# Attention of sixteen sequences: the slots of all engines in a new order

## What is computed

```python
cq = rms_norm(hidden_states @ w_qa.T, q_a_ln_w)                    # 192 columns
q = (cq @ w_qb.T).reshape(b, s, H, DQ).transpose(0, 2, 1, 3)       # 16 heads of 128 + 64
q_pe = q_pe * cos + rotate_half(q_pe) * sin
...
scores = jnp.einsum('bhqd,bhkd->bhqk', q_full, k_full) * scale
attn = jax.nn.softmax(jnp.where(causal, -jnp.inf, scores), axis=-1)
out = jnp.einsum('bhqk,bhkd->bhqd', attn, v)
return out @ w_o.T
...
x = _layernorm(x + rwkv_attention(x)); x = _layernorm(x + quantized_ffn(x))
x = _layernorm(x + latent_attention(x)); x = _layernorm(x + mixture_of_experts(x))
```

## Time and profile before

| | |
|---|---|
| median of 3 runs | 2410.62 us (2408.71 to 2412.27) |
| the profiled execution | 2416.53 us, span 2414.8 us |
| mean granted TensorE clock | 0.904 |
| TensorE, VectorE, ScalarE, GpSimd busy | 84%, 68%, 43%, 32% of the span |
| the attention phase, from its first scores to the next phase's first load | 1094.31 to 2054.26 us |

### The profile page before, as it was taken

The page is one execution under the profiler, slowest core; times in us unless marked ns, Lnnn a source line. Parts: engine busy times, 40 slices in busy tenths (PEclk is TensorE's granted clock), DMA queues, the critical chain, the costliest instruction groups (busy, mean ns, idle before and its releaser), DMA issues. The chain is left out here.

```text
span 2414.8 us, 36391 instructions
## 1 busy us (share of the span) xinstructions
PE 2026.7 (84%) x12368; PEld 1797.3 (74%) x12368; DVE 1650.5 (68%) x4500; ACT 1029.0 (43%) x2673; POOL 780.7 (32%) x701
## 2 busy tenths in 40 slices
PE   7999999999999699879998888888888884677850
PEld 5788878778787588748888888887888874567740
DVE  7876776677775465527788888888888885235428
ACT  5433433333332233226655555555555552225530
POOL 1222223222232000013344444444444445003552
PEclk9999999999999799969999999999998997788655
DMA  3100000000000344340000000000000000414656
GB/s 122 44 27 27 1 27 1 27 27 1 27 18 1 118 140 140 99 147 6 14 26 29 18 17 17 16 15 15 16 15 15 11 12 14 126 35 93 145 86 204
DMA packets 105975, 117.24 MB, mean 49 GB/s; under 512 B 17879, under 2 KB 97819, under 8 KB 105152
## 3 DMA queue, kind: packets, MB, share of 16 engines
q1 hardware_dynamic: 93504, 106.80, 14.3%
q0 software_dynamic: 12288, 8.11, 2.3%
HBM read 75.44 MB, written 55.53 MB: 54 GB/s over the span
## 5 line engine op out<-in xcount | busy, mean ns | idle before, releaser
L209 POOL TENSOR_TENSOR rwkv_gate<-rwkv_key,rwkv_gate 128x512 f32<-128x512 f32 x128 | 205.8, 1608 | 566.3 <-DVE rwkv_key L391 566.3
L1162 POOL TENSOR_TENSOR mla_w_raw<-mla_w_raw,mla_row_inv 128x512 f32<-128x512 f32 x192 | 199.1, 1037 | 351.4 <-DVE mla_row_inv L1478 350.6
L1293 ACT ACTIVATE mla_w_raw<-mla_w_raw,mla_least 128x256 f32<-128x256 f32 (+1 forms) x512 | 227.4, 446 | 85.6 <-DVE mla_least L1462 62.2
L276 ACT ACTIVATE rwkv_gate<-rwkv_r 128x512 f32<-128x512 f32 x128 | 76.4, 597 | 416.6 <-DVE rwkv_o_low L328 416.6
L377 DVE TENSOR_TENSOR rwkv_kv<-rwkv_v,rwkv_key 128x512 f32<-128x512 f32 x128 | 88.0, 688 | 176.5 <-PE rwkv_v L426 117.3
L1462 DVE CUSTOM_DVE_ANT_0 mla_w_raw<-mla_score,mla_mask 128x256 f32<-128x256 f32 (+1 forms) x512 | 156.5, 351 | 47.3 <-PE mla_score L1845 47.2
L443 PE MATMUL rwkv_out<-rwkv_w_high,rwkv_o_high 128*128 128x256 f32 x512 | 144.9, 283 | 35.6 <-DVE rwkv_o_low L328 35.6
L383 DVE TENSOR_TENSOR_SCAN rwkv_state<-rwkv_decay_w,rwkv_kv 128x256 f32<-128x256 f32 x256 | 163.4, 681 | 4.1
L1845 PE MATMUL mla_score<-mla_k_high,mla_q_high 128*128 128x256 f32 (+1 forms) x512 | 158.1, 309 | 0.0
L2200 POOL DMA_INDIRECT sums<-moe_y_rows,moe_e_rows x64 | 92.2, 1440 | 203.7 <-ACT moe_y_rows L2277 142.7
L1309 ACT ACTIVATE mla_p_high<-mla_turn 128x512 fp32r<-128x512 f32 x192 | 112.9, 588 | 84.5 <-PE mla_turn L1854 83.0
(11 more groups left out here) (371 smaller groups left out, 6647.1 us busy)
## 6 DMA issues: line engine op xcount, KB each, us to landing
moe_w_raw<-in_experts SPq DMA_DIRECT2D x32, 384.0 KB, 3.8
rwkv_w_raw<-in_rkvo SPq DMA_DIRECT2D x16, 512.0 KB, 3.3
moe_y_in<-sums SPq DMA_DIRECT2D x32, 256.0 KB, 3.0
sums<-ffn_empty SPq DMA_DIRECT2D x14, 512.0 KB, 7.8
slots<-ffn_empty SPq DMA_DIRECT2D x8, 722.5 KB, 6.4
moe_e_rows<-slots SPq DMA_DIRECT2D x32, 180.6 KB
mla_w_raw<-in_mla_heads SPq DMA_DIRECT2D x4, 1280.0 KB, 7.3
rwkv_x_in<-in_x_t SPq DMA_DIRECT2D x16, 256.0 KB, 4.3
```

The lines of the kernel that those rows point to most:

```text
L209: nc.gpsimd.tensor_tensor(gate[:, c % 2, :], key[:, c % 2, :], gate[:, c % 2, :], ALU.mult).then_inc(gated_done, 1)
L1162: nc.gpsimd.tensor_tensor(unit, unit, row_inv[:, v % PR, 0:len(heads)].rearrange("p (h a) -> p h a", a=1) .to_broadcast([P, len(heads), ke ...
L1293: last = nc.scalar.activation(probs[:, v % PR, i * keys:(i + 1) * keys], masked[:, v % 2, i * keys:(i + 1) * keys], ACT.Exp, bias=least[:, ...
```

## The change

The same instructions run per sequence, in another order. Each turn in `TURNS` may now carry the mark `late`. TensorE does in a slot: the probability turn, the scores, the early turns, the weighted sums, the late turns, and last the projection. What ScalarE, VectorE and GpSimd do with a late turn or a projection, they do at the start of the next slot (`late_turns`, `projected`). The latents move from slots 8 and 9 to 8 and 10, read in slots 9 and 11. The router's transposes and logits come one sequence later (`routed` and `logits`: -2), its 26 steps stand in slots 3 to 11, and the scatters in slots 0 to 7 of the sequence after. y1 moves to slot 8, y0 to slot 10, layer norm to slots 9 to 11. The residual rows and the rows of the sum (`x_res`, `y_rows`) have two buffers each. The loop runs over one sequence more.

```diff
-TURNS = (("q1", 0, 0), ("q1", 1, 1), ("q1", 2, 2), ("q1", 3, 3), ("k", 0, 3), ("q0", 0, 4), ("q0", 1, 5),
-         ("y1", 0, 5), ("q0", 2, 6), ("places", 0, 6), ("x", 0, 7), ("q0", 3, 9), ("routed", 0, 9), ("cq", 0, 10),
-         ("logits", 0, 11), ("y0", 0, 11))
-AHEAD = {"q1": 0, "k": 1, "q0": 1, "x": 2, "cq": 2, "y0": 0, "y1": -1, "routed": -1, "logits": -1, "places": -2}
+TURNS = (("q1", 0, 0), ("routed", 0, 0, "late"), ("q1", 1, 1), ("q1", 2, 2), ("logits", 0, 2, "late"), ("q1", 3, 3),
+         ("k", 0, 4), ("q0", 0, 5), ("q0", 1, 6), ("q0", 2, 7), ("x", 0, 7, "late"), ("q0", 3, 8),
+         ("y1", 0, 8, "late"), ("places", 0, 9, "late"), ("y0", 0, 10, "late"), ("cq", 0, 11, "late"))
+AHEAD = {"q1": 0, "k": 1, "q0": 1, "x": 2, "cq": 2, "y0": 0, "y1": -1, "routed": -2, "logits": -2, "places": -2}
 UNSPLIT = ("y0", "y1", "places")
 FIRST_TURNS = (("x", 0, 0), ("cq", 0, 0), ("k", 0, 0), ("x", 0, 1), ("q0", 0, 0), ("q0", 1, 0), ("q0", 2, 0),
                ("q0", 3, 0), ("cq", 0, 1))
-def slot_turns(seq, v):
-
-    return [(kind, index, seq + AHEAD[kind]) for kind, index, at in TURNS
-            if at == v and 0 <= seq + AHEAD[kind] < NSEQ and (seq < NSEQ or AHEAD[kind] < 0)]
+def slot_turns(seq, v, late):
+
+    return [(kind, index, seq + AHEAD[kind]) for kind, index, at, *when in TURNS
+            if at == v and (when == ["late"]) == late and 0 <= seq + AHEAD[kind] < NSEQ
+            and (seq < NSEQ or AHEAD[kind] < 0)]
 def turned_in(m):
@@ -883,8 +884,10 @@
 ALL_TURNS = list(FIRST_TURNS)
-for of_slot in range(SLOTS * (NSEQ + 2)):
-    ALL_TURNS += turned_in(of_slot) + slot_turns(*divmod(of_slot, SLOTS))
+for of_slot in range(SLOTS * (NSEQ + 3)):
+    ALL_TURNS += turned_in(of_slot)
+    for is_late in (False, True):
+        ALL_TURNS += slot_turns(*divmod(of_slot, SLOTS), is_late)
 TURN_AT = {t: n for n, t in enumerate(ALL_TURNS)}
 SPLITS = [sum(t[0] not in UNSPLIT for t in ALL_TURNS[:n + 1]) for n in range(len(ALL_TURNS))]
...
@@ -1041,6 +1044,19 @@
             return not isinstance(seq, int) or seq > 0
+        def late_turns(seq, v):
+
+            return slot_turns(*divmod(SLOTS * seq + v - 1, SLOTS), True) if seq + v > 0 else []
+
+        def projected(seq, v):
+
+            of, at = divmod(SLOTS * seq + v - 1, SLOTS)
+            if of < 0 or not exists(of + (1 if at < 8 else 2)) or at in (9, 11):
+                return None, None
+            if at < 8:
+                return ("abs" if at % 4 < 2 else "pe"), 8 * (of + 1) + at
+            return "latent", 2 * (of + 2) + (at - 8) // 2
+
         def slot_before(seq, v, back):
...
@@ -1116,12 +1132,12 @@
                     sp.wait_ge(turn_filled, TURN_AT["x", 0, seq + 1] + 1)
                     sp.dma_start(x_rows[:, :, :], seq_rows(x2, seq + 2)).then_inc(rows_in, 16)
-                if v == 9 and exists(seq):
-                    if late(seq):
-                        sp.wait_ge(res_added, 2 * seq)
-                    sp.dma_start(x_res[:, :, :], seq_rows(x2, seq)).then_inc(res_in, 16)
-                if v == 9 and exists(seq - 1):
-                    store(seq - 1)
+                if v == 0 and exists(seq - 2):
+                    store(seq - 2)
+                if v == 1 and exists(seq):
+                    if seq >= 2:
+                        sp.wait_ge(res_added, 2 * (seq - 1))
+                    sp.dma_start(x_res[:, par, :, :], seq_rows(x2, seq)).then_inc(res_in[par], 16)
             over_sequences(slot)
             sp.wait_ge(stored, 16 * NSEQ)
@@ -1180,22 +1196,20 @@
                 rope_sum(2 + c, 1, c)
             def slot(seq, par, v):
+                kind, n = projected(seq, v)
+                if kind == "latent":
+                    latent_rstd(n)
                 m, of, v1 = slot_before(seq, v, 1)
                 if m >= 0:
                     scale_probs(m, v1)
-                if v in (2, 3, 6, 7) and exists(seq + 1):
-                    tile, c = v // 4, v % 4 - 2
-
-                    pool.wait_ge(turn_filled, TURN_AT[f"q{tile}", 3, seq] + 1)
-                    rope_sum(4 * (seq + 1) + 2 * tile + c, tile, c)
-                if v in (8, 9) and exists(seq + 2):
-                    latent_rstd(2 * (seq + 2) + v - 8)
-                if v == 7 and exists(seq - 1):
+                if kind == "pe":
+                    of, tile, c = n // 8, n % 8 // 4, n % 4 - 2
+                    pool.wait_ge(turn_filled, TURN_AT[f"q{tile}", 3, of - 1] + 1)
+                    rope_sum(4 * of + 2 * tile + c, tile, c)
+                if v == 10 and exists(seq - 1):
                     norm_rstd(seq - 1)
-                if v >= 9 and exists(seq - 2):
-                    scatter(seq - 2, v - 9)
-                if v < 5 and exists(seq - 3):
-                    scatter(seq - 3, v + 3)
+                if v < 2 * TOPK and exists(seq - 3):
+                    scatter(seq - 3, v)
             def scatter(of, i):
                 if i == 0:
@@ -1206,8 +1220,6 @@
                     .then_inc(scattered[of % 2], 16)
             over_sequences(slot)
-            for i in range(3, 2 * TOPK):
-                scatter(NSEQ - 1, i)
             for par in range(2):
                 pool.wait_ge(scattered[par], 16 * 2 * TOPK * (NSEQ // 2))
...
@@ -1334,27 +1346,28 @@
             nc.scalar.activation(wr_part[0][:, :, :], wr_raw[:, :, :], ACT.Copy).then_inc(wr_high, 1)
             def slot(seq, par, v):
+                for t in late_turns(seq, v):
+                    if t[0] not in UNSPLIT:
+                        split_turn(*t)
+                kind, n = projected(seq, v)
+                if kind == "abs":
+                    of, tile, c = n // 8, n % 8 // 4, n % 4
+                    act.wait_ge(turn_filled, TURN_AT[f"q{tile}", 3, of - 1] + 1)
+                    q_abs(n, tile, c)
+                elif kind == "latent":
+                    squares_of(n)
                 m, of, vt = slot_before(seq, v, TURN_LAG)
                 if m >= 0:
                     probs_high(m, vt)
                 m, of, vs = slot_before(seq, v, SUM_LAG + 1)
                 if m >= 0 and completes(vs):
                     sums_high(of, vs)
-                if v in (8, 9) and exists(seq + 2):
-                    squares_of(2 * (seq + 2) + v - 8)
-                turns = [t for t in slot_turns(seq, v) if t[0] not in UNSPLIT]
-                for t in turns[:1]:
+                for t in slot_turns(seq, v, False):
                     split_turn(*t)
                 if exists(seq):
                     exps(seq, v)
-                if v in (0, 1, 4, 5) and exists(seq + 1):
-                    tile, c = v // 4, v % 4
-                    act.wait_ge(turn_filled, TURN_AT[f"q{tile}", 3, seq] + 1)
-                    q_abs(8 * (seq + 1) + 4 * tile + c, tile, c)
                 if v == 6 and exists(seq + 1):
                     values_high(seq + 1, 1 - par)
-                for t in turns[1:]:
-                    split_turn(*t)
             over_sequences(slot)
...
@@ -1486,14 +1499,15 @@
             def add_residual(kind, seq):
                 n, tile = TURN_AT[kind, 0, seq], int(kind[1])
                 dve.wait_ge(turn_filled, n + 1)
-                dve.wait_ge(res_in, 16 * (seq + 1))
-                if tile == 0 and late(seq):
-                    dve.wait_ge(normed, seq)
-                nc.vector.tensor_tensor(y_rows[:, tile, :], turn_ps[n % TURN_BANKS][:, 0:D], x_res[:, tile, :], ALU.add)\
+                dve.wait_ge(res_in[seq % 2], 16 * (seq // 2 + 1))
+                if tile == 0 and seq >= 2:
+                    dve.wait_ge(normed, seq - 1)
+                row = y_rows[:, seq % 2, tile, :]
+                nc.vector.tensor_tensor(row, turn_ps[n % TURN_BANKS][:, 0:D], x_res[:, seq % 2, tile, :], ALU.add)\
                     .then_inc(res_added, 1)
                 dve.wait_ge(res_added, 2 * seq + tile + 1)
-                nc.vector.bn_stats(stats[:, tile, :], y_rows[:, tile, :]).then_inc(turn_read, 1)
+                nc.vector.bn_stats(stats[:, tile, :], row).then_inc(turn_read, 1)
...
@@ -1665,53 +1679,51 @@
             def slot(seq, par, v):
                 routed = exists(seq - 2)
+                for t in late_turns(seq, v):
+                    turn(*t)
+                kind, n = projected(seq, v)
+                if kind == "pe":
+                    of, tile, c = n // 8, n % 8 // 4, n % 4 - 2
+                    q_turn(4 * of + 2 * tile + c, n + 1, tile, c)
                 if exists(seq):
                     mask_scores(seq, v)
-                if routed and v == 0:
-                    route_choice(seq - 2, 1)
-                if routed and v < 6:
-                    route_choice(seq - 2, 3 * v + 2)
+                if routed and 3 <= v < 9:
+                    route_choice(seq - 2, 3 * v - 8)
+                if routed and v in (9, 10):
+                    route_weight(seq - 2, 3 * v - 8)
+                if routed and v == 11:
+                    route_slots(seq - 2, 25)
```

(61 more changed lines are left out.)

19 lines of the change are left out of this document (6 added, 13 removed).

## The result

The kernel after takes 2377.53 us (2371.33 to 2379.08) against 2410.28 us (2408.71 to 2412.27) on the same chip, a ratio of 0.985 [0.9837, 0.9863]. Its profiled execution took 2377.56 us with a span of 2375.8 us. The forecast was 2390 us, faster, in a range of 2330 to 2418. By the medians the gain is 32.8 us.

The account below looks back on a forecast made before the run. VectorE's run (41.5 us) plus TensorE's cq and slots 0 to 2 (15.4) bound a sequence: 56.9, with 2.2 for the clock 59.1. Eleven sequences -8, edges -12: 2390 us from 2410.6, range 2330 to 2418.

Parts of the forecast that it names:

- The run: VectorE without rest from the mask of slot 3 to the latent in slot 11: 41.5 us.
- The stalls: VectorE's router steps held by GpSimd in slots 3 to 11: 8.3 us a sequence, against 5.6 before.
- step 12: Router step on VectorE under the scatter of slot 6: loses 0.75 us.
- steps 3, 6, 15 and 18: Router steps in slots 3, 4, 7 and 8 run into GpSimd's rope sum: lose 1.25, 0.9, 1.1 and 0.9 us.
- TensorE's part: From cq through slots 0 to 2 to the scores of slot 3: 15.4 us; TensorE's own work 48.2 us a sequence.
- The clock: Half clock in slots 0 to 2 costs between nothing and 5.4 us a sequence; 2.2 taken.
- The rival by the clock: Wait before cq puts TensorE at 1.2 GHz through slots 0 to 2: 62.3 us a sequence, 2426 us; chance 0.12.
- Edges: Sequences 0, 1, 2, 14, 15 and the tail: -3, -6, -1, -3, -3 and +4 us, together -12.
- Smaller stalls: VectorE's router steps in slots 3 to 11 are held less: 2329 us, or 2345 without the rope part alone; chance 0.27.
- No change: VectorE's lag and the edges cancel: 60.5 to 61.3 us a sequence; chance 0.12.
- Scatters that hold the tensor_tensor steps: GpSimd's scatters after the rope sum also hold VectorE's router steps: +3, so 62.1 us a sequence, 2424 us; chance 0.07.
- Signs: Long held router steps, no wait before latents, 3 to 4 us before cq, period 59 us, tail 47 us.

Follow-up runs that it names:

- The two subtractions: Two more 128x512 VectorE subtractions a sequence added to the kernel after: in slot 5 2389.89 us, in a separate run in slot 1 2383.02 us.
- filler kernel: The kernel after with 12 unread matmuls of 512 columns on TensorE in front of the wait before cq: 2345.44 us, 0.9708.
- twice in slot 5: The kernel after with two more 128x512 subtractions on VectorE in slot 5 of every sequence: 2389.89 us, 0.9888.
- two scatters in slot 8: Kernel with rope sum before scaling, router steps 20-26 in slots 0-2, slot 11's latent early; its last two scatters moved one slot earlier: 2298.58 us.

## Why the prediction was right, and where its sizes were off

**What bounds it.** Right: VectorE's unbroken run in slots 3 to 11, the cq wait behind it, TensorE's slots 0 to 2. The two subtractions moved from slot 1 to slot 5 show it. The latents' waits are gone, and with the projections back in their old place one returns and a sequence is 2.1 to 3.6 us longer. No run moves the router's steps or the latents alone back, so what each part of the change is worth isn't shown.

**The run.** 41.5 us forecast, 39.0 measured. The stalls are 7.0 us, not 8.3 (medians less shortest of the held steps): step 12, for which I had 0.75, costs nothing; steps 3, 6, 15 and 18 cost 0.99, 0.83, 1.08 and 0.78 where I had 1.25, 0.9, 1.1 and 0.9. Each of the other mechanisms was there. Step 12's was not: it does stand under the scatter of slot 6, as forecast, and isn't held by it.

```profile
1566.37 0.99 POOL L1217 DMA_INDIRECT slots<-mla_x_out,mla_slot_now  x1 [0.16 <-issue]
1566.55 0.18 DVE L1580 TENSOR_SCALAR mla_choice<-mla_choice 128x64 f32<-128x64 f32 x1
```

The same step took 1.62 us in the earlier trace rows, where it began 0.51 us into the scatter and GpSimd's scaling followed 0.02 us behind that. Which of the two differences matters isn't shown. The other 1.2 us of the run are VectorE's own work, 32.0 in place of 33.2.

**TensorE's part.** 55.0 - 39.0 = 16.0 us at full clock, 15.4 forecast. Its waits: 0.88 in slot 4 (0.9), 0.4 in slot 7 (1.6), 1.3 in slot 8 (2.0), 2.94 before cq (3.7). VectorE was less late than I had it, and TensorE's own work is greater: 55.0 less 5.7 us of waits and filler in the filler kernel is 49.3, not 48.2.

**The clock.** 2.2 us forecast, 3.2 measured. The rival by the clock had its mechanism right and its size wrong: in the kernel after the lower level does come with each wait of 2.9 us before cq, some 7 us of it at the head of sequence 9 (1591 to 1598), and such a microsecond costs nearly the half that it was priced at; but it would have decided only from 8.8 us on. (In its price 1.5 x 11 over the edges' 12 makes 4.5, not 4.8, which changes nothing.) The Trainium skill ("TensorE: Matmul & The Clock Gate", section "HAM oscillation") says that a wait that comes again in each round can put the clock back in each round. The kernel after agrees, with 58.2 us a sequence, and filled with work the wait does no such thing (55.0). But the wait alone doesn't decide: in twice in slot 5 sequences 4, 8 and 12 begin at full clock behind waits of 2.9 us. What else it takes isn't shown.

**Sum.** 56.9 + 2.2 = 59.1 forecast, 55.0 + 3.2 = 58.2 measured: the run's 2.5 too many outweigh 0.6 and 1.0 too few. Over eleven sequences that is -16.5 us, not -8. This is the term that was mis-sized, most of it by the stalls and VectorE's own work.

**Edges.** -19.5, not -12. Sequence 1 came at 47.8 (48 to 50). Sequence 2 gave 4.0 where I had 1: the clock held through it (PEclk 1.00 against 0.91 in the kernel before). That it has no scatters, my reason, gives nothing: it takes 55.0 us, as the filler kernel's sequences with scatters do. Sequence 15 gave 4.6 (3), sequence 14 2.0 (3), the tail took 1.6 (4, within its 0 to 8). The 2.9 us in the next phase were in no term; what gives them isn't shown.

**The rivals.** Smaller stalls, 2329 to 2345, came only in part, 7.0 us for 8.3; but for step 12 they stand where they were worked out. No change needed 60.5 us or more. Scatters that hold the tensor_tensor steps: the steps end with the rope sum (step 15, the latest, at 1572.59, 0.13 into the scatter of 1.00 us behind it), step 12 runs through one, and two scatters in slot 8 lengthened nothing.

**Signs.** L1547 1.18 (1.2 or more), L1557 0.99 (about 1.1), L1588 1.49 (1.5), no wait before the latents, tail 44.7 (47), period 58.2 (59).

## What to carry to other kernels

Follow the engine that never rests from the wait that starts its run to the reader of its last result; only work inside that run counts, and the same instruction a slot outside it is free. A wait of some 3 us on TensorE costs itself and, in nearly every sequence here, slow work behind it, so take it away, or fill it where it stands and nowhere else. After each cut read the waits again: here each of three cuts put something new in the way (other router steps beside the moved rope sum, y0 behind the latent, a scatter ahead of a root). Moving that scatter gave 0.8 us a sequence, some 9 of the last 14 us; another 1.5 is a slow head of one sequence that didn't come again, and 1.6 lie in sequence 0, from a cause not shown.
